# Self-attention on one Trainium2 core: GpSimd's copy of 16 rows placed ahead of its scaling of the probabilities

## What is computed

```python
Wdkv = x @ latent_w + latent_b                               # 72 channels
q = jnp.einsum('btc,hcl->bhtl', x, Wd_w) + Wd_b[None, :, None, :]
scores = jnp.einsum('bhtl,bsl->bhts', q, Wdkv) / jnp.sqrt(d_head)
scores = jnp.where(causal, scores, -jnp.inf)
attn = jax.nn.softmax(scores, axis=-1)
y = jnp.einsum('bhts,bsl->bhtl', attn, Wdkv)
z = jnp.transpose(y, (0, 2, 1, 3)).reshape(b, t, h * 72)
x = layernorm(x + z @ out_w + out_b)
```

## Time and profile before

| | before |
|---|---|
| median of three runs | 3089.1 us (3088.31 to 3090.59) |
| the profiled execution | 3090.44 us |
| its span, first to last instruction | 3088.0 us |
| PE busy | 3060.8 us, 99% |
| DVE busy | 2255.0 us, 73% |
| ACT busy | 2139.6 us, 69% |
| POOL busy | 1579.4 us, 51% |
| mean granted clock of PE | 0.999 |

### The profile page before, as it was taken

One profiled execution on the slowest core, in us unless ns is written; L12 is line 12 of the kernel. 1 busy time (PEld: TensorE's weight loads), 2 busy tenths in 40 slices (PEclk: granted clock), 3 DMA queues, 4 the chain that ended last, 5 costly groups with the idle time before them and its releaser, 6 DMA issues. The chain is left out here.

```text
span 3088.0 us, 72815 instructions
## 1 busy us (share of the span) xinstructions
PE 3060.8 (99%) x22529; PEld 2875.2 (93%) x22529; DVE 2255.0 (73%) x6595; ACT 2139.6 (69%) x6949; POOL 1579.4 (51%) x2918
## 2 busy tenths in 40 slices
PE   9999999999999999999999999999999999999998
PEld 7999999999999999999999999999988888889998
DVE  7888888888888777777878788787765555554665
ACT  8888888888888878777878777787844444442222
POOL 5676676766776765333333333333456666652000
PEclk9999999999999999999999999999999999999999
DMA  5455555544444461111111111111354454534333
GB/s 162 135 158 163 156 158 159 150 129 125 119 130 131 130 211 45 46 49 63 46 49 59 52 46 56 56 45 49 110 144 100 99 116 106 113 52 96 123 122 102
DMA packets 209569, 321.06 MB, mean 104 GB/s; under 512 B 36416, under 2 KB 143040, under 8 KB 208224
## 3 DMA queue, kind: packets, MB, share of 16 engines
q1 hardware_dynamic: 184672, 283.59, 30.6%
q0 software_dynamic: 24576, 33.57, 6.5%
HBM read 125.20 MB, written 75.50 MB: 65 GB/s over the span
## 5 line engine op out<-in xcount | busy, mean ns | idle before, releaser
L1200 POOL TENSOR_SCALAR ca_prob<-ca_prob,ca_inverse 128x120 f32<-128x120 f32 x1024 | 354.6, 365 | 616.3 <-DVE ca_inverse L1499 614.2
L875 ACT ACTIVATE sa_prob<-sa_prob,sa_shift 128x128 f32<-128x128 f32 (+1 forms) x1024 | 454.1, 462 | 0.0
L1440 ACT ACTIVATE ca_prob<-bank,ca_shift 128x120 f32<-128x120 f32 x1024 | 353.9, 366 | 1.7 <-DVE ca_shift L1493 0.5
L937 DVE CUSTOM_DVE_ANT_0 sa_prob<-bank,sa_mask 128x128 f32<-128x128 f32 (+1 forms) x1024 | 303.4, 351 | 5.9 <-issue 5.2
L599 POOL TENSOR_SCALAR sa_prob<-sa_prob,sa_inverse 128x128 f32<-128x128 f32 x512 | 193.7, 378 | 200.7 <-DVE sa_inverse L949 187.3
L139 PE MATMUL bank<-sa_kvT_b,sa_q 112*128 112x128 f32 (+1 forms) x1024 | 260.4, 280 | 0.0
L981 DVE TENSOR_TENSOR sa_pT_lo<-bank,sa_pT_hi 128x384 fp32r<-128x384 f32 x512 | 258.0, 543 | 0.2 <-ACT sa_pT_hi L864 0.2
L601 POOL TENSOR_SCALAR sa_prob<-sa_prob,sa_inverse 128x256 f32<-128x256 f32 x512 | 252.7, 494 | 0.0
L137 PE MATMUL bank<-sa_kvT_a,sa_q 128*128 128x128 f32 (+1 forms) x1024 | 249.4, 280 | 1.1 <-DVE sa_shift L937 0.9
L1932 POOL DMA_INDIRECT mid_acc<-ex_out,ex_to_tokens x112 | 190.3, 1699 | 98.9 <-DVE ex_out L2244 65.7
L864 ACT ACTIVATE sa_pT_hi<-bank 128x384 fp32r<-128x384 f32 x512 | 223.1, 495 | 1.1 <-PE bank L755 1.1
(11 more groups left out here) (274 smaller groups left out, 11918.3 us busy)
## 6 DMA issues: line engine op xcount, KB each, us to landing
sa_q<-sa_q_tile SPq DMA_DIRECT2D x125, 288.0 KB
sa_q<-sa_q_tile SPq DMA_DIRECT2D x157, 112.0 KB
mid_x2T<-ca_x2T SPq DMA_DIRECT2D x32, 512.0 KB, 3.0
ex_sx<-mid_x2T SPq DMA_DIRECT2D x32, 512.0 KB
sa_q<-sa_q_tile SPq DMA_DIRECT2D x297, 32.0 KB
sa_xT_raw<-in_xT SPq DMA_DIRECT2D x32, 256.0 KB, 3.0
sa_q<-sa_q_tile SPq DMA_DIRECT2D x32, 256.0 KB
sa_x_res<-in_x SPq DMA_DIRECT2D x32, 256.0 KB
```

The costliest lines, as they stand in the source:

```text
L875: act.activation(prob[:, r, hh, cols], prob[:, r, hh, cols], ACT.Exp, bias=shift[:, r, n:n + 1], scale=-1.0, accum_out=total[:, r, n:n + 1 ...
L937: dve.tensor_tensor_reduce(out=prob[:, r, hh, cols], in0=SC[hh][:, t * T:t * T + (t + 1) * P], in1=mask[:].rearrange("p a s -> p (a s)")[: ...
L1200: ins = pool.tensor_scalar(prob[:, r, t, hh], prob[:, r, t, hh], inverse[:, r, n:n + 1], 1.0, ALU.mult, ALU.mult)
L1440: act.activation(prob[:, r, t, hh], SC[g % 2][:, n * S:n * S + S], ACT.Exp, bias=shift[:, r, n:n + 1], accum_out=total[:, r, n:n + 1]).the ...
```

## The change

POOL's copy for step m - 10 stands at the head of the slot, ahead of the four scalings for step m - 7. Its wait for the scalings now means those of the slot before. Three waits of POOL for its own last instruction are added or made general: after the split of x, after x1 and after the inverse root.

```diff
@@ self_attention, gpsimd, slot
                 pool.wait_ge(head_dup, h + 1)
+            g = m - PL
+            if slot_exists(J, g):
+                r = g % RING
+                need(pool, p_done, at_most(upto_slot(J, m - 1 - IL, 2), 2 * B * NP))
+                need_alone(pool, yhi_done, upto_slot(J, g), spare_pool)
+                own = slice(int(packed(g) and g % QUAD < 2), 2)
+                pool.tensor_scalar(y_lo[AT:AT + REST, y_at(J, g), own], f32(y_hi[0:REST, r, own]), 1.0, 1.0, ALU.mult, ALU.mult).then_inc(ydup_done, 1)
+                need(pool, ydup_done, upto_slot(J, g))
             g = m - IL
             if slot_exists(J, g):
                 r = g % RING
...
                     pool.tensor_scalar(prob[:, r, hh, P:3 * P], prob[:, r, hh, P:3 * P],
                                        inverse[:, r, 2 * hh + 1:2 * hh + 2], 1.0, ALU.mult, ALU.mult).then_inc(p_done, 1)
-            g = m - PL
-            if slot_exists(J, g):
-                r = g % RING
-                need(pool, p_done, at_most(upto_slot(J, m - IL, 2), 2 * B * NP))
-                need_alone(pool, yhi_done, upto_slot(J, g), spare_pool)
-                own = slice(int(packed(g) and g % QUAD < 2), 2)
-                pool.tensor_scalar(y_lo[AT:AT + REST, y_at(J, g), own], f32(y_hi[0:REST, r, own]), 1.0, 1.0, ALU.mult, ALU.mult).then_inc(ydup_done, 1)
-                need(pool, ydup_done, upto_slot(J, g))
             c, u = m // GROUP, m % GROUP
...
             if u in X_SPLIT and group_exists(J, c + 1):
                 split_x(J, c + 1, X_SPLIT.index(u))
+                need(pool, xlo_done, upto_row(J, c + 1, X_SPLIT.index(u)))
...
-                if x1_at(J, m)[i] == X1_LATE:
-                    pool.wait_ge(x1_done, upto_row(J, c, i, TT))
+                need(pool, x1_done, upto_row(J, c, i, TT))
...
                 pool.tensor_tensor(rstd[:, i], var_eps[:, i], half[:], ALU.pow).then_inc(rstd_done, 1)
+                need(pool, rstd_done, upto_row(J, c, i))
```

## The result

| | before | changed |
|---|---|---|
| median | 3090.6 us (3088.3 to 3091.6, 5 runs) | 3102.9 us (3102.4 to 3103.9, 5 runs) |
| ratio | | 1.0042, 95% interval 1.0032 to 1.0053 |
| the profiled execution | 3090.4 us | 3103.9 us |
| its span | 3088.0 us | 3101.4 us |

The change makes the kernel 12.3 us slower, where 7.4 us were forecast. The direction and the kind of loss were right; the size was too small by two fifths. The forecast counted from 3089.1 us, the median of the first three runs; the 3102.9 us lie above its 3094 to 3100 and at the upper end of the outer range, 3103. The profiled spans differ by 13.4 us. One execution of a later experiment (the meetings moved), which took 3731.7 us at a mean granted clock of 0.75, is left out; all others are within 0.2% of their medians.

A forecast was written before the change was run, and what follows sets the result against it. PE was taken to bound the kernel, POOL's time counting only where PE waits. Losses of 0.9 + 4.5 + 0.6 + 1.1 + 0.3 = 7.4 us on 3089.1 gave 3096.5 us, range 3090 to 3103.

The forecast's parts named there:

- What bounds the kernel: Whole kernel: PE sets the pace, busy 3060.8 of 3088.0 us; at most some 2 us of POOL-caused waits can go.
- the ordinary slot's room: Ordinary self-attention slot: first transposes come 4.18 us after y_hi, leaving 1.8 us slack and no cost.
- Part (1): Every slot: scalings now wait for y_hi and the copy; chain from y_hi to second head's transposes is 2.69 us.
- part (2): Slot 9 of each group: PE loses 0.02 to 0.18 us each time, 0.9 us in all.
- Part (3): Where POOL's instructions meet DVE's line 1008 weight staging: scalings are held, 4.5 us over seven places, bounds 0 to 7.7.
- Part (4): Start, where ACT and DVE also split weights: two slots lose 0.35 and 0.27 us, 0.6 us.
- Part (5): Drain after slot 256, where PE's slots are short: losses of 0.56, 0.36 and 0.14 us, 1.1 us.
- Part (6): Two slots 12: each loses 0.18 us, 0.3 us with rounding.
- Part (7): POOL's added waits for itself: 0.22 us each, inside the other figures or in slots with room, so nothing extra.
- A: Rival: meetings fall on DVE or beside and tight slots have room; 0 to 5 us lost, about 3091.5; chance 0.32.
- B: Rival: late transposes delay ACT and the next y_hi, so losses spread; adds 11 us, 3107; chance 0.14.
- C: Rival: faster through fewer POOL and DVE meetings and smaller starting losses; 3082.5 us at very best; chance 0.04.

The follow-up runs named there:

- the meetings moved: Changed kernel with cross-attention weight staging started in slot 44, repeated every 8 slots, instead of 40 and 6: 3106.1 us against 3090.4 for the kernel before.
- One wait less: Changed kernel without the copy's wait for the last scaling in nine of sixteen slots of groups 3 to 14: 3101.2 us against 3088.5 before.
- the waits alone: Kernel before, its order kept, with the three added POOL waits for itself: 3091.1 us against 3090.4, ratio 1.0001.
- the copy made twice: Changed kernel with POOL's copy issued twice in every slot, each waited for: 3162.0 us against 3090.9 for the kernel before, ratio 1.0227.
- the second trace of the changed kernel: Changed kernel run once more without any edit: 3104.0 us against 3088.5 for the kernel before, ratio 1.0048.

## Why the prediction was right or wrong

**What bounds the kernel** held. PE has nothing to win in this stage, and a PE loss isn't caught up. "POOL's idle time turns into waiting for y_hi" held (206.0 against 15.8 us), and so did the ordinary slot's room.

**Part (1), the chain of 2.69 us, is the step that failed.** In the rows of slot 9 it is 0.29 + 0.61 + 0.23 + 1.63 + 0.05 = 2.81 us (749.51 to 752.32). The distance from y_hi to the first transposes is as before, 2.30 us (749.51 to 751.81, before 527.45 to 529.75). What made 0.24 us out of my 0.04:
- y_hi to copy, 0.18 us. I took it from a slot whose last instructions were the scalings. In slot 9 the copy comes behind a split with one of the added waits, and there it is 0.29 us. One wait less brought 0.18 back.
- 0.23 us where I used 0.22.
- The second head follows the first by three starts of 0.11 us, 0.33 us, where I used 0.35.
- A term that I left out: after the wait the second transpose starts 0.165 us behind the first instead of 0.11, so PE loses 0.05 us more than the delay of the first transpose. The last scaling to PE, 0.05 us, was right.

Together they are 0.2 us, 7% of the chain, but the slack that it was set against was -0.04 us, and it was multiplied by fourteen. With 0.24 us instead of 0.04 in part (2) slot 9 costs 3.4 us instead of 0.9.

**Part (3), slot 1.** My own figure for slot 1 without a meeting was a loss of 0.10 us, and I used it only to price the meeting. It belonged in the sum fourteen times, 1.4 us. Measured it is 0.30 us, the same chain twice passed with the pair between and the same terms too small, so 4.2 us in all. This is the largest single gap. (The prediction is uneven here: its terms without the meetings add up to 2.9 us, its walk without them gave 3.7, and it doesn't say which slots have the 0.8.) The meetings themselves: eight instead of seven places, 3.1 instead of 4.5 us. The hold is as the earlier trace rows had it. In the slot 9 that I used as the example POOL starts first and is held:

```profile
176.68 0.37 POOL L607 TENSOR_SCALAR sa_prob<-sa_prob,sa_inverse 128x128 f32<-128x128 f32 x1 [0.23 <-POOL sa_y_lo L600]
177.02 1.30 POOL L609 TENSOR_SCALAR sa_prob<-sa_prob,sa_inverse 128x256 f32<-128x256 f32 x1
177.29 0.68 DVE L1009 SCALAR_TENSOR_TENSOR early_st_lo<-early_st_raw,early_st_hi 128x512 fp32r<-128x512 f32 x1
...
178.38 0.55 PE L756 MATMUL bank<-all_ident,sa_prob 128*128 128x128 f32 x3 [0.46 <-POOL sa_prob L609]
```

The second scaling starts 0.27 us ahead of DVE's instruction and ends at 178.32, 0.48 us after 177.84, which is 0.13 us before DVE's end. It was the dearer of my two cases, 1.15 us behind this slot. The Trainium skill (SBUF — State Buffer, "SBUF: two separate sides") has the lock itself, and this row agrees with it; with its rule that the first to start keeps the ports the row doesn't agree. DVE's sixteen rows of line 1009 take 0.68 us each, so DVE is never the one held in this trace, while each of them holds a scaling.

**Part (4), the start,** was 0.6 us for two slots and measured 2.2. I looked for late slots in the rows before, but the one at 69 us was already late then (PE waits 0.35 and 0.25 us for the scaling), and after the change it waits 0.78 and 0.25. The old order in the first 32 slots takes nearly all of it away. **Part (5), the drain,** was right (1.1, measured 1.0). Part (6) didn't show.

**Part (7)** said that the added waits are inside the figures. That holds for POOL's time and for the old order, as the waits alone show. It is wrong for the lag of the next copy, 0.11 us.

**Luck.** The two slots that recur cost 7.6 us where the sum had 0.9. That the total isn't further off is owed to the meetings, priced 1.4 us too high, and to the two losses of the kernel before, 0.7 us.

**The rivals.** A (the cover holds) falls with the result. B (lateness spreads) falls with the copy made twice and the old order in slots 1 and 9: roomy slots lose nothing. C was excluded by the result. The sign that I had named for B, PE waits of 0.1 us or more in every group, did come, and B was wrong all the same: the waits stand in slots 10 and 2 of every group, and each is local. A better sign would have been losses in roomy slots. Of the other signs, the places came as forecast (40 more waits) with twice the time (13.8 us). The copy follows y_hi by 0.18 us in 117 of 256 slots, by 0.28 or 0.29 us in 73 and later in 66, by 1.7 us in slot 1. Late copies were named as the sign of a wrong chain, and slot 1 is where the sum lacked one. My sum with 0.1 us more for the chain stood in the text as 11.8 us. That was the honest size of the uncertainty, since every slack near zero occurs in nearly every group; I took the middle, and every link that I had from an easier row turned out longer.

## What to carry to other kernels

When a wait moves ahead of work that a saturated engine needs, compare the new chain with the distance to its consumer slot by slot, and ask of the slot before what still stands in the queue. A slack within 0.1 or 0.2 us of zero that recurs in every period isn't free: take the links of the chain from rows in the very same situation, multiply by the count, and put the missing tenth in the sum rather than in the range. Where the consumer's row counts as busy, look at the length of the merged row (0.82 to 1.06 us) and at the waits of the weight loads, which here name the releaser and nearly the whole loss.

## What the runs showed of the hardware

- Semaphore waits in front of a GpSimd instruction can cost lead even when they have long been fulfilled. The trace's records of the queue's semaphore instructions, which the views above leave out, show where. With two waits in front of the copy both stand in one such instruction together with a semaphore increment, and the copy follows y_hi by 0.18 us (117 copies of the changed kernel). With three the wait for y_hi stands alone, and the instruction with the two old waits and the increment comes behind it: 0.29 us (70 copies). In the kernel before, 13 copies have a lone third wait, without an increment, behind that instruction, and the lag is 0.18 us.
- A wait for the instruction just before costs 0.08 to 0.09 us when the waiting instruction carries it itself (832.82 to 832.91; 72 cases in the kernel before) and 0.22 us or more when a separate semaphore instruction carries it, together with a second wait and an increment (714.98 to 715.21). That the increment takes the 0.13 us would fit both this and the lag of the copy, but no run removed it alone.
- A scaling releases PE after 0.05 us in every place of the changed kernel from 100 us on where PE's second head waited for it, and the matmul behind the released one starts 0.165 instead of 0.11 us later.
- A GpSimd instruction that starts up to 0.43 us ahead of a DVE instruction with two SBUF inputs is held by it until 0.13 us before its end (a scaling of 0.37 us takes 1.35 us). Others that start 0.33 to 0.35 us ahead, and end as DVE starts, aren't held. In the run with the waits alone two DVE rows are themselves longer, 0.76 us, behind a copy that began 0.39 us earlier. Why the start of the row doesn't decide is open.
- In the changed kernel's profile PE's granted clock is 0.98 in the first 100 us. It is 1.00 there in the second trace of the changed kernel, which is as slow, and 0.98 in that with the waits alone, whose time is that of before. So it doesn't explain the loss.
